# Attention with a two-step graph network over 32 heads: values projected for two heads at once, three sets of value buffers, and a new order of calls

## What is computed

```python
xn = layer_norm(x, gamma_in)
q = (xn @ Wq).reshape(b, n, HEADS, DHEAD).transpose(0, 2, 1, 3) * scale
k, v = ...
sim = jnp.where(causal_mask, mask_value, jnp.einsum('bhid,bhjd->bhij', q, k))
attn = jax.nn.softmax(sim, axis=-1)
out = jnp.einsum('bhij,bhjd->bhid', attn, v)
adj = jnp.clip(attn.reshape(b * HEADS, n, n) + eye, 0.0, 1.0)
deg = jnp.sum(adj, axis=-1, keepdims=True)
feats = v.reshape(b * HEADS, n, DHEAD)
for l in range(2):
    h = feats @ gnn_w[l] + gnn_b[l]
    h = jnp.einsum('bij,bjd->bid', adj, h) / deg
    feats = gelu(h + feats)
out = out + (feats @ lin_w + lin_b)
return layer_norm(out @ Wo, gamma_out)
```

## Time and profile before

| what | value |
|---|---|
| three runs, median | 1515.64 us (1507.6 to 1525.04) |
| profiled execution, its own time | 1520.77 us |
| its span, first to last instruction | 1519.0 us |
| granted TensorE clock over the span | 0.969 of full speed |
| PE, PEld (weight loads), DVE, ACT, POOL busy | 93%, 73%, 78%, 66%, 24% |

### The profile page before, as it was taken

The page is one execution under the profiler, slowest core; times in us unless marked ns, Lnnn a source line. Parts: engine busy times, 40 slices in busy tenths (PEclk is TensorE's granted clock), DMA queues, the critical chain, the costliest instruction groups (busy, mean ns, idle before and its releaser), DMA issues. The chain is left out here.

```text
span 1519.0 us, 29014 instructions
## 1 busy us (share of the span) xinstructions
PE 1411.2 (93%) x9944; PEld 1105.3 (73%) x9944; DVE 1190.5 (78%) x3496; ACT 1009.8 (66%) x2376; POOL 366.2 (24%) x474
## 2 busy tenths in 40 slices
PE   5999999999999999999999999999679999999895
PEld 4677788878887788878888788777456566666663
DVE  5378788878787777878888888875888888878875
ACT  3366667776776766767676777666455787778573
POOL 2013221221122211322223222232323322222211
PEclk8589999999999999999999999999898999999999
DMA  5012211121111211121111211220300000000100
GB/s 135 0 32 48 64 29 29 33 52 29 29 32 39 43 29 29 32 50 32 29 32 38 45 29 29 64 47 1 94 22 19 22 22 19 22 18 22 29 12 21
DMA packets 40668, 53.30 MB, mean 35 GB/s; under 512 B 11678, under 2 KB 23882, under 8 KB 40522
## 3 DMA queue, kind: packets, MB, share of 16 engines
q1 hardware_dynamic: 40522, 51.46, 15.2%
HBM read 9.89 MB, written 1.05 MB: 7 GB/s over the span
## 5 line engine op out<-in xcount | busy, mean ns | idle before, releaser
L1147 ACT ACTIVATE t<-PS 128x512 f32<-128x512 f32 (+3 forms) x384 | 188.9, 492 | 141.5 <-PE PS L686 90.5
L1647 DVE TENSOR_TENSOR t<-t 128x512 fp32r<-128x512 f32 (+3 forms) x384 | 209.9, 553 | 35.5 <-ACT t L1148 32.4
L1148 ACT ACTIVATE t<-PS 128x512 fp32r<-128x512 f32 (+3 forms) x384 | 188.0, 489 | 0.0
L736 PE MATMUL PS<-t 128*128 128x512 f32 (+3 forms) x384 | 147.7, 385 | 21.8 <-ACT t L1181 21.6
L1304 ACT ACTIVATE t<-PS,t 128x128 f32<-128x128 f32 x256 | 113.2, 464 | 68.6 <-DVE t L1898 68.6
L657 PE MATMUL PS<-t 128*128 128x512 f32 (+3 forms) x384 | 144.0, 378 | 9.2 <-DMA t<-t 6.8
L1444 POOL TENSOR_TENSOR t<-t 128x256 f32<-128x256 f32 x64 | 39.3, 613 | 461.7 <-DVE t L1667 461.7
L683 PE MATMUL PS<-t 128*128 128x512 f32 (+3 forms) x384 | 146.9, 383 | 2.2 <-DMA t<-t 2.2
L1480 POOL TENSOR_TENSOR t<-t 128x16 f32<-128x16 f32 x32 | 92.8, 2900 | 232.5 <-DVE t L1748 232.5
L684 PE MATMUL PS<-t 65*128 65x512 f32 (+3 forms) x384 | 136.1, 354 | 0.0
L701 PE MATMUL PS<-t 128*66 128x512 f32 (+3 forms) x384 | 134.6, 351 | 0.1
(11 more groups left out here) (206 smaller groups left out, 3902.4 us busy)
## 6 DMA issues: line engine op xcount, KB each, us to landing
t<-t SPq DMA_DIRECT2D x184, 128.0 KB, 2.3
t<-t SPq DMA_DIRECT2D x62, 256.0 KB, 3.4
t<-in_c_rot SPq DMA_DIRECT2D x4, 512.0 KB, 5.2
t<-in_L_ffn_wqkv SPq DMA_DIRECT2D x2, 768.0 KB, 6.7
t<-in_L_attn_Wv SPq DMA_DIRECT2D x2, 512.0 KB, 7.0
out<-t SPq DMA_DIRECT2D x4, 256.0 KB, 2.3
t<-in_L_ffn_w SPq DMA_DIRECT2D x2, 341.0 KB
t<-in_L_attn_x SPq DMA_DIRECT2D x2, 256.0 KB, 3.0
```

The source lines that it names most:

```text
L736: e.matmul(dst, F2[:, jb, :], Eh[:, o:o + n], start=(jb == 0), stop=False)
L1147: e.activation(Es[:, k % NS, 0:n], b[:, 0:n], ACT.Exp).then_inc(a_es.up((t, k)), 1)
L1148: e.activation(Eh[:, o:o + n], b[:, 0:n], ACT.Exp).then_inc(a_eh.up((t, k)), 1)
L1647: e.tensor_tensor(El[:, o:o + n], Es[:, k % NS, 0:n], f32(Eh[:, o:o + n]), ALU.subtract).then_inc(d_el.up((t, k)), 1)
```

## The change

- `projv` projects two heads, t and t + 1, in even t only, with matmuls of 256 columns; `widen_v` cuts the weights of two heads in one go. Both halves c of the positions write the same columns of the two banks 6 and 7, so half 1 waits until DVE has read half 0 of both heads.
- The value buffers `VH`, `VL`, `vB`, `vW` have RV = 3 sets instead of 2.
- The calls in the loop stand in another order on PE, ACT, DVE and POOL. The first graph product of an even head waits for an older event, that of an odd one for the values of head t + 2.
- To make room, small tiles of the prologue are laid over `OFT`, and `wqkv0` over the queries and keys of the first layer. It is loaded after the last scores of head 30.

```diff
-        wqkv0 = tile(1536)
...
+        RV = 3
+        VH = [sb1([P, 8, 66], F32R) for _ in range(RV)]
+        VL = [sb1([P, 8, 66], F32R) for _ in range(RV)]
...
-        WR = [sb1([P, 2, P], F32R) for _ in range(2)]
+        WR = sb1([P, 2, 2 * P], F32R)
...
+        w0d, ini = OFT[:, 0:P], OFT[:, P:260].rearrange("p (a n) -> p a n", a=2)
+        LW, LBc, linw = OFT[0:DH, 260:388], OFT[0:DH, 388:516], OFT[0:DH, 516:580]
...
+        wqkv0 = tile(1536)
...
+            q.wait_ge(*p_sc[NH - 2, NTL - 1])
+            e.dma_start(wqkv0, I["L0_ffn_wqkv"][0]).then_inc(ld["wqkv0"], 16)
```

PE, `projv` and the wait of the first graph product:

```diff
             def projv(t, c):
-                if t >= NH:
-                    return
-                b, bk, w = t // HA, 6 + c, WR[t % RB]
+                if t >= NH or t % 2:
+                    return
+                b = t // HA
                 q.wait_ge(*d_turn[2 * b + c])
                 q.wait_ge(*w_wr[t])
-                if t == 0:
-                    q.wait_ge(*a_val["W", c])
-                elif t == 1:
-                    q.wait_ge(*a_lin[3 - c])
+                if c:
+                    q.wait_ge(*d_vb[t + 1, 0])
+                elif t == 0:
+                    q.wait_ge(*a_val["W", 1])
                 elif t == 2:
                     q.wait_ge(*d_o1[0, 1])
                 else:
-                    q.wait_ge(*d_y[t - 3, c])
+                    q.wait_ge(*d_y[t - 3, 1])
                 for k in range(4):
                     o = b * NT + (4 * c + k) * P
-                    dst = bank(bk)[:, k * P:(k + 1) * P]
-                    e.matmul(dst, xh[:, o:o + P], w[:, 0, :], start=True, stop=False)
-                    e.matmul(dst, xh[:, o:o + P], w[:, 1, :], start=False, stop=False)
-                    m = e.matmul(dst, xl[:, o:o + P], w[:, 0, :], start=False, stop=True)
+                    dst = bank(6, 2)[:, k * 2 * P:(k + 1) * 2 * P]
+                    e.matmul(dst, xh[:, o:o + P], WR[:, 0, :], start=True, stop=False)
+                    e.matmul(dst, xh[:, o:o + P], WR[:, 1, :], start=False, stop=False)
+                    m = e.matmul(dst, xl[:, o:o + P], WR[:, 0, :], start=False, stop=True)
                 m.then_inc(p_pv.up((t, c)), 1)
...
-                elif t + 1 < NH:
-                    q.wait_ge(*d_vb[t + 1, 1])
+                elif t % 2 and t + 2 < NH:
+                    q.wait_ge(*d_vb[t + 2, 1])
                 else:
                     q.wait_ge(*d_y[t - 2, 1])
```

ACT and DVE, `projv` (POOL's `widen_v` goes the same way):

```diff
                 q.wait_ge(*p_pv[t, c])
-                q.wait_ge(*w_n2[t - RB, 1])
-                q.wait_ge(*p_av[t - RB, 1])
                 q.wait_ge(*d_zero["ini"])
-                e.copy(vW[r][:, ks, :], pv[:, :, DH:P])
-                e.copy(VH[r][:, ks, 0:DH], pv[:, :, 0:DH]).then_inc(a_v.up((t, c)), 1)
+                for i in range(2):
+                    u, r = t + i, (t + i) % RV
+                    q.wait_ge(*w_n2[u - RV, 1])
+                    q.wait_ge(*p_av[u - RV, 1])
+                    e.copy(vW[r][:, ks, :], pv[:, :, i, DH:P])
+                    e.copy(VH[r][:, ks, 0:DH], pv[:, :, i, 0:DH]).then_inc(a_v.up((u, c)), 1)
...
-                q.wait_ge(*a_v[t, c])
                 q.wait_ge(ld["gb"], 32)
-                q.wait_ge(*d_pre[t - RB, 1])
-                e.tensor_tensor(VL[r][:, ks, 0:DH], pv[:, :, 0:DH], f32(VH[r][:, ks, 0:DH]), ALU.subtract).then_inc(d_vl.up((t, c)), 1)
-                e.tensor_tensor(vB[r][:, ks, :], pv[:, :, 0:DH], gb[:, 0:1, :].broadcast_to([P, 4, DH]), ALU.add).then_inc(d_vb.up((t, c)), 1)
+                q.wait_ge(*a_v[t + 1, c])
+                for i in range(2):
+                    u, r = t + i, (t + i) % RV
+                    q.wait_ge(*d_pre[u - RV, 1])
+                    e.tensor_tensor(VL[r][:, ks, 0:DH], pv[:, :, i, 0:DH], f32(VH[r][:, ks, 0:DH]), ALU.subtract).then_inc(d_vl.up((u, c)), 1)
+                    e.tensor_tensor(vB[r][:, ks, :], pv[:, :, i, 0:DH], gb[:, 0:1, :].broadcast_to([P, 4, DH]), ALU.add).then_inc(d_vb.up((u, c)), 1)
```

Of the order of calls the diff shows two lines of PE's loop, `smax(t + 1, 0)` and `scores(t, 4)`:

```diff
-                smax(t + 1, 0)
...
+                scores(t, 4)
+                smax(t + 1, 0)
```

More of the change, by code:

```diff
@@ L139, in program @@
         sb1([P, 4])
+        RB = 2
+        Q1, K1 = [None] * RB, [None] * RB
+        for i in range(RB):
+            Q1[i], K1[i] = sb1([P, NT], F32R), sb1([P, NT], F32R)
         WqD = area_qk[:, 0:HA * DH].rearrange("p (h d) -> p h d", h=HA)
@@ L191, in program @@
         HT0, qr0, tm, sq = (tile(n) for n in (NT + 2, 1024, 1024, 1024))
+        tile(2)
+        wqkv0 = tile(1536)
         wqkv, wo, w1, w2, b1, lnp, qks, tabl = [], [], [], [], [], [], [], []
@@ L259, in program @@
         norms_ += [("h", q) for q in range(5)] + [("h", 5), ("out", 4), ("h", 6), ("h", 7), ("out", 5), ("out", 6), ("out", 7)]
+        by_pair = [(t + i, c) for t in range(0, NH, 2) for c in range(2) for i in range(2)]
         p_turn = signal("p_turn", range(4))
@@ L264, in program @@
         p_proj = signal("p_proj", halves)
-        p_pv = signal("p_pv", halves)
+        p_pv = signal("p_pv", [(t, c) for t in range(0, NH, 2) for c in range(2)])
         p_max = signal("p_max", maxes)
@@ L281, in program @@
         a_q0 = signal("a_q0", range(2))
-        a_v = signal("a_v", halves)
+        a_v = signal("a_v", by_pair)
         a_row = signal("a_row", heads)
@@ L296, in program @@
         d_low = signal("d_low", halves)
-        d_vl = signal("d_vl", halves)
-        d_vb = signal("d_vb", halves)
+        d_vl = signal("d_vl", by_pair)
+        d_vb = signal("d_vb", by_pair)
         d_max = signal("d_max", maxes)
@@ L318, in program @@
         w_wd = signal("w_wd", heads)
-        w_wr = signal("w_wr", heads)
+        w_wr = signal("w_wr", range(0, NH, 2))
         w_n2 = signal("w_n2", halves)
@@ L836, in tensor @@
                     linear(0, 7)
-                scores(t, 3)
+                scores(t, 4)
+                smax(t + 1, 0)
+                smax(t + 1, 1)
                 tailT(t - 2, 1)
@@ L849, in tensor @@
                 scores(t, 5)
-                tail(t - 2, 1)
+                scores(t, 6)
                 smax(t + 1, 4)
@@ L853, in tensor @@
                     linear(3, 6)
-                scores(t, 6)
+                tail(t - 2, 1)
                 smax(t + 1, 5)
+                scores(t, 7)
+                smax(t + 1, 6)
                 projv(t + 1, 0)
-                graph2(t - 1, 11)
-                scores(t, 7)
+                av(t, 1)
                 av(t, 2)
                 av(t, 3)
+                scores(t, 8)
+                graph2(t - 1, 11)
+                scores(t, 9)
                 projv(t + 1, 1)
-                scores(t, 8)
-                smax(t + 1, 6)
+                smax(t + 1, 7)
                 av(t, 4)
-                smax(t + 1, 7)
+                scores(t, 10)
+                smax(t + 1, 8)
                 av(t, 5)
@@ L869, in tensor @@
                     linear(5, 7)
[L870 to L873, removed]
+                av(t, 6)
                 graph1(t, 0)
[L875 to L877 removed]
                 av(t, 9)
                 av(t, 7)
[L880 removed]
+                scores(t, 11)
+                smax(t + 1, 9)
                 graph2b(t - 1)
@@ L1235, in scalar @@
                 scores(t, 2)
-                scores(t, 3)
+                share(t - 1, 1)
                 if t == 0:
@@ L1239, in scalar @@
                 tailT(t - 2, 0)
-                share(t - 1, 1)
+                scores(t, 3)
                 if t == 0:
@@ L1248, in scalar @@
                 scores(t, 6)
+                scores(t, 7)
                 projv(t + 1, 0)
                 av(t, 0)
-                scores(t, 7)
+                scores(t, 8)
+                hopend(t - 1, 1)
+                scores(t, 9)
                 projv(t + 1, 1)
-                scores(t, 8)
+                scores(t, 10)
                 if t == 0:
                     linear(4, 6)
-                scores(t, 9)
-                scores(t, 10)
                 scores(t, 11)
+                gelu_table(t)
+                feats(t, 0)
                 proj(t + 2, 0, 2)
-                hopend(t - 1, 1)
-                feats(t, 0)
-                gelu_table(t)
-                share(t, 0)
                 proj(t + 2, 1, 3)
                 av(t, 1)
+                share(t, 0)
+                mrow(t + 1)
                 gelu2(t - 1)
@@ L1774, in vector @@
             q.wait_ge(*own.now())
-            for i in range(RB):
+            for i in range(RV):
                 e.tensor_copy(VL[i][:, :, 64:66], ini[:, 0:1, 0:2].broadcast_to([P, 8, 2]))
                 e.tensor_copy(VH[i][:, :, 64:66], ini[:, 1:2, 0:2].broadcast_to([P, 8, 2]))
+            for i in range(RB):
                 e.tensor_copy(K2[i][64:65, :], ini[64:65, 1, 0:1].broadcast_to([1, NT]))
@@ L1819, in vector @@
                     began(1)
+                scores(t, 1)
+                share(t - 1, 1)
+                scores(t, 2)
                 smax(t + 1, 0)
-                scores(t, 1)
```

(18 more changed lines are left out.)

89 lines of the change are left out of this document (34 added, 55 removed).

## The result

| | before | after |
|---|---|---|
| median, lowest to highest | 1516.43 us (1507.6 to 1525.04, 4 runs) | 1494.92 us (1493.26 to 1497.43, 4 runs) |
| ratio | 1 | 0.9862, 95% interval 0.9833 to 0.9892 |
| profiled execution: time, span | 1520.77, 1519.0 us | 1495.98, 1494.2 us |
| granted TensorE clock | 0.969 | 0.974 |

A forecast was written before the change was run, and what follows sets the result against it. PE, busy 97% of the turns through the heads, was taken to bound them. -38 - 6.8 + 6 + 2 + 9 + 7.5 + 0.4 = -20 us gave 1500.8, on the median's scale 1496 us; range 1470 to 1516.

The forecast's parts named there:

- wide matmuls: Value projection on PE: 24 wide matmuls replace 48 narrow ones per pair of heads, 38 us off.
- transfers: Maxima of the next head on PE: standing later in the turn, they stop waiting for doubling DMAs, 6.8 us off.
- the head's turn: Second graph product to first exponentials: PE's cover falls from 7.0 to 5.9-6.0 us, 0.25 us a turn, 7.5 us on.
- round trip: Second half of values waits for ACT's copies and DVE's reads: 0.4 us in each of 15 odd turns, 6 us on.
- graph product: First graph product waits for the second half of the values: 0.15 us, 15 times, 2 us on.
- norm turns: Odd turns with a layer norm: DVE's statistics and scaling between the halves show 1.1 us, 8 times, 9 us on.
- start: Prologue and turn 0: head 1's projection leaves turn 0, 5 us off; prologue projects two heads, 5.4 on; net +0.4 us.
- no waits: Rival: the new order hides the waits and PE keeps the most work; 1471 us, chance 0.19.
- Bare round trip: Rival: DVE late at both halves, PE stands there and at the first graph product; up to 81 us, 1552, chance 0.12.
- Wide matmuls cost more: Rival: a wide matmul of the projection costs up to 0.175 us, gain 18 us, time 1516, chance 0.08.
- New order waits elsewhere: Rival: 0.65 us more a turn, at the minimum before the row of maxima or the exponentials; 1516 us, chance 0.08.
- Clock comes back early: Rival: turn 0's low clock ends early, some 23 us would go at the full level; 1473 us, chance 0.07.

The follow-up runs named there:

- narrow pairs: Changed kernel with each 256-column matmul of the value projection made as two of 128, all else as changed: 1528.04 us, ratio 1.0069.
- second pair of executions: The kernel before and the changed kernel, each run once more with nothing altered: 1511.91 and 1492.36 us.
- first pair: The profiled executions of the kernel before and of the changed kernel: 1520.77 and 1495.98 us.
- best variant: Changed kernel with the scaling of the layer norms on DVE moved behind the second half of the values: 1488.8 us, ratio 0.9827.

## Why the prediction was right

It said 1496 us with a range of 1470 to 1516; it came to 1494.9. The terms, by the sums of the runs:

| term | forecast, us | measured, us | from |
|---|---|---|---|
| wide matmuls | -38 | -36.2 | last two sums: 905.1 - 941.3 |
| new order alone: transfers and the head's turn | -6.8 + 7.5 = +0.7 | -4.9 | 927.5 - 932.4 |
| pairing of heads without norm: round trip, graph product, first half | +6 + 2 = +8 | +13.8 | 941.3 - 927.5 |
| norm turns | +9 | +5.0 | 910.1 - 905.1 |
| sum of 30 turns | -20.3 | -22.3 | 910.1 - 932.4 |
| start | +0.4 | -5.7 in the profile | 82.7 - 88.4 |
| behind the turns | 0 | +3.1 in the profile | |

- **Wide matmuls.** Right. Starts are 0.119 apart over the stream, for 0.118 forecast, and by PE's starts the whole difference of the two sums lies at the lines of the projection (85.8 us in 30 turns for 49.5). The narrow ones paid for their weights, not for their columns. The Trainium skill (TensorE: Matmul & The Clock Gate, LDWEIGHTS) says that a load takes its columns divided by 1.2 in ns, whatever the rows: an estimate of 107 ns for 128 columns and 55 for 66, and the trace agrees with 0.112 and 0.06. The Trainium skill's 81 ns for a stream of 128 (same page, Back-to-back issue gap), by which an estimated 19 us would have been won, is refuted for these matmuls by the runs: 36 us.
- **The head's turn, +7.5.** This step failed. I had reasoned that a cover that falls from 7.0 to 5.9 us shows as 0.25 us a turn. The old code in the new order has turns of 30.9 us, as long as the kernel before has where nothing waits for a transfer, so there is no such loss. The transfers' waits go, and only some 2 us of the 6.8 come back, in turns 1, 6, 7 and 30.
- **The round trip, +6 and +2.** The bare time, 2.7 us, was right, and so was the cover, to a tenth: the wait itself is about 0.1, not 0.4. But the term is too small. In turn 11 of the narrow pairs against the old code in the new order, PE's starts show 0.3 us more at the first half, 0.2 at the second and 0.1 at the graph product, of the 0.92 us that pairing costs a pair (13.8 / 15). The rest is spread over small places, mostly score tiles. The first of these, over 4 us of the 13.8, is a wait that the prediction doesn't have: the first half needs both banks free, and so DVE's second sum of the same turn. (In turn 1, where the code waits there for another event, the loss is absent: the first matmul starts 0.06 behind the one before, for 0.34 in the other odd turns.) At the other two the stop itself is a tenth or less, and the rest is that the matmul behind it starts 0.2 us later and not 0.12, which I read as a weight load that isn't hidden. So two terms of the sum were off by 5 or 6 us each, in opposite directions, and the norm's by 4 more; the total of the turns is right to 2 us by luck in good part.
- **Norm turns, +9.** The mechanism was right, at the place named, in the turns named; the price is 0.8 us in turns 19 to 25 and 0.3 to 0.4 in turns 3, 5, 27 and 29, for a forecast of 1.1. Moving the scaling takes it away.
- **Start.** Of the two parts one can be seen: the row of maxima of head 0 is 5.9 us later (39.2 for 33.3; forecast 5.4), and 4.7 in the second pair of executions. The other, 5 us off turn 0, can't: turn 0 took 43.5 us for 55.1 in the first pair and 42.2 for 38.4 in the second, by where the clock was low.
- **Behind the turns** I had put nothing. PE's windows just behind the turns show a clock of 0.88 for 0.93 before, but the low stretches there lie elsewhere in every run, and in the second pair this part was 0.8 us shorter with the change (499.2 for 500.0). So the 3.1 us are not shown to be the change's.

The rivals: *no waits* would have needed a sum of 887, and the best variant has 905. *Bare round trip*: not so here, since PE stands for a tenth at the second half; the experiment shows what it costs when bare, 1565 for the 1552 that I gave it, the falls of the clock included. *Wide matmuls cost more*: no, 0.119. *New order waits elsewhere*: no, alone it gains 4.9 us. *Clock comes back early*: it did in the profile, by 18 us (66 for 84), and took part of the 11.6 us off turn 0, for the 23 forecast; but it does so in the kernel before as well.

## What to carry to other kernels

Widening matmuls that only pay for their weight loads gives what the distances of starts say, if the buffers that are then shared are read in time; the order of calls was worth 5 us before this change and 47 with it, so the two can't be judged apart. When a resource is shared by two halves, compare the chain (last matmul, copies, reads) with the work between, and look at what runs ahead of the readers on their engine: moving one scaling by a few lines gave 5 us, and moving the same round trip off the prologue's path brought the first row of maxima 4.8 us forward. When a call is made to write more banks, list anew what each of them was last read for: the first half's wait was missed that way. Terms found by setting a chain against a cover of nearly the same length are worth a few tenths a turn either way, and should carry that as their range.

## What the runs showed of the hardware that I had not expected

- With a stop of PE of 2.7 us the clock may fall to 1.2 GHz, in ten of fifteen turns with the same stop: for 3.4 us in eight of them and 6.8 in two. It also fell behind stops of 1.59 and 1.71 us, and not behind those of 1.43 and 1.49. The stop of 0.7 us in the norm turns of the changed kernel never brought it down (window of the changed kernel from turn 21 to the last, clock third from the right).

```profile
700.00:992.00 292.00, 281.53 (x1802) 230.94 (x1801) 248.78 (x815) 202.43 (x457) 74.67 (x109) 1.00 0.18 40
```

- The low clock at the start lasts differently from one execution to the next: in the kernel before it lasted from 26 to 84 us with PE busy for 47.26 of the 48 us from 36 to 84, and in another execution it ended at 43.
- Two maxima put some 2 us early on PE alone (and score tile 2 behind a hop tile) cost 20 us, nearly the whole gain, though PE's longest wait for their transfers was 0.9 us.
